# Wave attention: the value products of four heads in one call, a fourth sine of key tile 0 summed on TensorE, and that tile's sums in two banks by turns

## The chip, the cores and the metric

One core of a Trainium2 chip runs the whole kernel. The metric is the device time in microseconds (us). Engines are named as in the profile: PE is TensorE (PEld its weight loads), DVE is VectorE, ACT is ScalarE, POOL is GpSimd, SP is SyncE.

## What is computed

Four blocks one after the other on x of shape (8, 512, 128): a first attention, a mixture of experts, a second attention, the mixture again. The change touches the first attention, whose weights are sigmoids of a sum of five sines of the scores:

```python
sim = jnp.einsum('bhid,bhjd->bhij', q, k) / jnp.sqrt(hd) / temp      # 8 x 16 heads, 512 x 512
scores = 0
for fi, freq in enumerate([31.0, 37.0, 41.0, 43.0, 47.0]):
    scores = scores + a[fi] * jnp.sin(TWO_PI * sim / freq + p[fi])   # a, p: one number per head
w = jax.nn.sigmoid(scores)
w = w / (jnp.sum(w, axis=-1, keepdims=True) + 1e-10)
out = jnp.einsum('bhij,bhjd->bhid', w, v)
```

## The kernel before

`wave_attention` works through 128 heads (n), in 32 groups of four (`HG`; g is the group, h the head in it). A head's scores lie as 128 key rows by 2048 columns: four key tiles (kt) of 512 queries. The order on each engine is written out by hand; a loop (`Fori`) takes two groups in a pass, and the engines meet at semaphores only.

- **TensorE**, per head n: scores of head n+2, tiles 0 and 1 (`make_scores`, L667, one 128x512 matmul a tile, into psS); then the sum of the first three sines (`PE_F`) in psA: for each sine f and tile one fp32 matmul with a diagonal matrix that holds the head's factor (L704; a matmul in fp32 is two passes in the trace, so x8 is four matmuls). After f = 0 come the scores of head n+2, tiles 2 and 3. Behind head 0 of a group stand the value products of heads 0 and 1 of the group before, behind head 2 those of heads 2 and 3 (`values`, L679): 9 output rows a head, at psO rows 0, 32, 64 or 96, the two heads by turns.
- **ScalarE**, per head n: five sines over 2048 columns (L772), each when its angle is there; behind the third and the fifth it takes half of head n+2's scores out of psS (L737), the first angle. Behind head 0 it does the four sigmoids of the group before (L754), behind head 3 the copy of psO (L761). For head 0 of a group it makes the last angle too (L747).
- **VectorE**, per head n: the angles of head n+1 (`make_angles`: a multiply-add, L822, called a turn, for each of the angles 1 to 4, and a shift, L847, called a cut, for all five), then the fourth and fifth sine of head n added to psA's sums (`add_sine`, L860): two additions of 1024 columns each, from psA to score and from score to score.
- **GpSimd** makes the diagonals (L641), three a head, from identity and parameters, and copies V and the parameters of the next group.

The semaphores that matter: `sine` (ACT to PE and DVE), `summed` (a half of psA is complete: PE to DVE and POOL), `added` (an addition is done: DVE to PE, which may overwrite that half of psA, and to ACT), `s_ps` and `s_ready` (psS full: PE to ACT; taken: ACT to PE), `weighed` (a sigmoid is done: ACT to PE), `out_ps` (value products done), `used` (a sine was summed). Below, an engine's "head 1" is its work for a head with h = 1.

Of the kernel before, what the change touches and what calls it, by code (L numbers as in the profile page):

```python
# [11 lines left out]
ALU = mybir.AluOpType  # L12
# [3 lines left out]
P = 128  # L16
B, L, D = 8, 512, 128
H, HD = 16, 8
QT = L // P
NT = B * QT  # L20
HG = 4
NG = B * H // HG
# [2 lines left out]
FREQS = (31.0, 37.0, 41.0, 43.0, 47.0)  # L25
NF = len(FREQS)
PE_F = 3
TWO_PI = 2.0 * float(np.pi)
E, HID = 8, 512
NE = E + 1  # L30
# [504 lines left out]
def wave_attention(nc, sb, ps, sem, a, V, ident, dram, params, bound):  # L535
# [11 lines left out]
    N = QT * L  # L547
    HALF = N // 2
    SR, AR = 2, 2 * HG
    DV_F = NF - PE_F  # L550
    ADDS = 2 * DV_F

    C_SPS, C_SREADY, C_TURNED, C_LAST, C_CUT, C_SINE, C_USED, C_SUMMED = 2 * 2 * HG, 2, 2 * HG * (NF - 1), 2 * HG, 2 * HG * NF, NF, 2 * PE_F, 4
    C_ADDED, C_DIAG, C_OUT, C_TAKEN, C_STORED = 2 * HG * ADDS, 2 * HG, 2, 1, 16
    with ExitStack() as c:
# [7 lines left out]
        score = sb(c, "score", [P, AR, N])  # L563
        par = sb(c, "par", [P, 2, 3, HG * NF])
        far = sb(c, "far", [P, 1], I32)
        diag = sb(c, "diag", [P, 2, PE_F, P])
        og = sb(c, "og", [P, L])
        Vg = sb(c, "Vg", [P, 2, QT, HG, VW])
        psS = ps(c, "psS", [P, 2, L])
        psA = ps(c, "psA", [P, QT, L])  # L570
        psO = ps(c, "psO", [P, L])
        qk_loaded = [sem(c, f"qk_loaded{i}") for i in range(2)]
        s_ps = sem(c, "s_ps")
# [50 lines left out]
        @block.gpsimd  # L624
        def _(pool):

            pool.tensor_copy(par[:, 0, :, :], params[:, 0, :, :]).then_inc(par_ready, 1)
            with pool.Fori(0, B) as b:
                for gi in range(GPB):
                    g, u = b * GPB + gi, gi % 2  # L630

                    pool.wait_ge(out_ps, g - 1 + C_OUT)
                    pool.sem_inc(pool_step, 1)
                    pool.tensor_copy(Vg[:, u, :, :, :], V[:, bass.ds(g, 1), :, :, :]
                                     .rearrange("p a q h d -> p (a q) h d")).then_inc(v_ready, 1)
                    pool.wait_ge(par_ready, g + 1)
                    for h in range(HG):

                        pool.wait_ge(summed, (g * HG + h) * 2 - 2 + C_SUMMED)
                        for f in range(PE_F):  # L640
                            ins = pool.tensor_tensor(diag[:, h % 2, f, :], ident[:],  # L641
                                                     par[:, u, 1, h * NF + f:h * NF + f + 1]
                                                     .to_broadcast((P, P)), ALU.mult)
                        ins.then_inc(diag_ready, 1)
                        if h == 1:

                            pool.wait_ge(added, g * HG * ADDS + C_ADDED)
                            pool.wait_ge(cut, g * HG * NF + C_CUT)
                            pool.sem_inc(pool_step, 1)
                            pool.tensor_copy(par[:, 1 - u, :, :], params[:, (gi + 1) % GPB, :, :]  # L650
                                             ).then_inc(par_ready, 1)
            pool.wait_ge(out_ps, NG - 1 + C_OUT)
            pool.tensor_copy(Vg[:, 0, :, :, :], V[:, NG, :, :, :]).then_inc(v_ready, 1)

        @block.tensor
        def _(pe):
            for credit, n in ((s_ps, C_SPS), (s_ready, C_SREADY), (turned, C_TURNED), (last_turned, C_LAST), (cut, C_CUT), (sine, C_SINE),
                              (used, C_USED), (summed, C_SUMMED), (added, C_ADDED), (diag_ready, C_DIAG),
                              (out_ps, C_OUT), (out_taken, C_TAKEN),
                              (out_stored, C_STORED)):  # L660
                pe.sem_inc(credit, n)

            def make_scores(n, u, h, half):
                pe.wait_ge(s_ready, n * 2 + half + C_SREADY)
                for k in range(2):
                    kt = half * 2 + k
                    mm = pe.matmul(psS[:, k, :], kp[:, u, h, kt * P:(kt + 1) * P], qp[:, u, h, :],  # L667
                                   start=True, stop=True)
                mm.then_inc(s_ps, 1)

            def values(g, slot, heads):
                if heads[0] == 0:
                    pe.wait_ge(v_ready, g + 1)
                    pe.wait_ge(out_taken, g + C_TAKEN)
                pe.wait_ge(weighed, g * HG + heads[-1] + 1)
                for kt in range(QT):
                    for h in heads:
                        row = h * (P // HG)
                        mm = pe.matmul(psO[row:row + VW, :],  # L679
                                       Vg[:, slot ^ 1, kt, h, :],  # L680
                                       score[:, slot * HG + h, kt * L:(kt + 1) * L],
                                       start=(kt == 0), stop=(kt == QT - 1), skip_group_check=True)
                if heads[-1] == HG - 1:
                    mm.then_inc(out_ps, 1)

            def pair(gg, last):
                for u in range(2):
                    g = gg * 2 + u
                    for h in range(HG):
                        n = g * HG + h  # L690
                        more = not (last and u == 1 and h >= HG - 2)
                        nu, nh = (u, h + 2) if h < HG - 2 else (1 - u, h + 2 - HG)
                        if more:
                            if nh == 0:
                                pe.wait_ge(qk_loaded[nu], (gg + 1 + u) * 32)
                            make_scores(n + 2, nu, nh, 0)
                        pe.wait_ge(diag_ready, n + 1 + C_DIAG)
                        for f in range(PE_F):
                            pe.wait_ge(sine, n * NF + f + 1 + C_SINE)
                            for kt in range(QT):  # L700
                                if f == 0 and kt % 2 == 0:

                                    pe.wait_ge(added, n * ADDS - ADDS + kt // 2 + 1 + C_ADDED)
                                mm = pe.matmul(psA[:, kt, :], diag[:, h % 2, f, :],  # L704
                                               wave[:, h % 2, f, kt * L:(kt + 1) * L],
                                               start=(f == 0), stop=(f == PE_F - 1), skip_group_check=True)
                                if f == PE_F - 1 and kt % 2 == 1:
                                    mm.then_inc(summed, 1)
                            if f < PE_F - 1:
                                mm.then_inc(used, 1)  # L710
                            if more and f == 0:
                                make_scores(n + 2, nu, nh, 1)
                        if h in (0, 2):
                            values(g, 1 - u, (h, h + 1))

            pe.wait_ge(qk_loaded[0], 32)
            for h in range(2):
                for half in range(2):
                    make_scores(h, 0, h, half)
            with pe.Fori(0, NG // 2 - 1) as gg:  # L720
                pair(gg, False)
            pair(NG // 2 - 1, True)
            for h in (0, 2):
                values(NG, 1, (h, h + 1))

        @block.scalar
        def _(act):
# [77 lines left out]
        def _(dve):  # L805
# [19 lines left out]
            def make_angles(n, u, h, gs, general):  # L825
# [4 lines left out]
                for f in range(NF + 1):  # L830
                    if f < PE_F - 1:
                        dve.wait_ge(used, (n - 2) * (PE_F - 1) + f + 1 + C_USED)
                    elif f == PE_F - 1:
                        dve.wait_ge(summed, (n - 2) * 2 + 2 + C_SUMMED)
                    elif f < NF:
                        dve.wait_ge(added, n * ADDS - 2 * ADDS + 2 * (f - PE_F + 1) + C_ADDED)
                    if (f or general) and (f < NF - 1 or (f == NF - 1 and (general or h not in ACT_LAST))):
                        make_turns(n, u, h, f, general)
                    if f:
# [7 lines left out]
                        dve.tensor_scalar(angle[:, h % 2, f - 1, :], at, 32 - FRAC, None,  # L847
                                          ALU.logical_shift_left).then_inc(cut, 1)

            def add_sine(n, u, h, f):  # L850
                dve.wait_ge(sine, n * NF + f + 1 + C_SINE)
                for half in range(2):
                    cols = slice(half * HALF, (half + 1) * HALF)
                    if f == PE_F:
                        dve.wait_ge(summed, n * 2 + half + 1 + C_SUMMED)
                        other = psA[:, half * 2:half * 2 + 2, :].rearrange("p a n -> p (a n)")
                    else:
                        dve.wait_ge(added, n * ADDS + (f - PE_F - 1) * 2 + half + 1 + C_ADDED)
                        other = score[:, u * HG + h, cols]
                    dve.scalar_tensor_tensor(  # L860
                        out=score[:, u * HG + h, cols], in0=wave[:, h % 2, f, cols],
                        scalar=par[:, u, 1, h * NF + f:h * NF + f + 1], in1=other,
                        op0=ALU.mult, op1=ALU.add).then_inc(added, 1)

            def pair(gg, last, general):
                for u in range(2):
                    g = gg * 2 + u
                    for h in range(HG):
# [6 lines left out]
                            make_angles(n + 1, nu, nh, ng * 2 * HG, general)  # L875
                        if h == 0:
                            dve.wait_ge(out_ps, g + C_OUT)
                        for f in range(PE_F, NF):
                            add_sine(n, u, h, f)


            dve.tensor_scalar(far[:], bound[:], FAR * min(FREQS) / HD, None, ALU.is_ge).then_inc(far_ready, 1)
# [1036 lines left out]
```

## Time and profile before

| | |
|---|---|
| median of 3 runs | 4277.99 us (4274.96 to 4281.38) |
| the profiled execution | 4281.09 us, span 4279.3 us |
| PE busy | 3602.2 us (84%), 27092 instructions |
| DVE busy | 3409.0 us (80%), 4519 instructions |
| ACT busy | 2868.0 us (67%), 2433 instructions |
| POOL busy | 1271.6 us (30%), 918 instructions |
| L704, matmuls into psA | 1445.5 us |
| L772, sines | 1181.2 us |
| L679, value products | 239.8 us |

Wave attention fills about 110 to 2085 us of the span. In the profile a group of instructions has its busy time, the mean duration of one, and behind the bar the idle time of its engine just before it, with what ended it. In a timeline each row is a start, a length, the engine, the line and the instruction; equal instructions one behind the other are one row, with their count, and a row's length runs to the end of its last instruction, which overlaps the next row's start a little. So lengths of work are taken below from start to start.

### The profile page before, as it was taken

Reading aid. Unit: us, or ns where it says so; the run is one execution under the profiler, and the core shown is the slowest. Engines: PE = TensorE matmul, PEld = TensorE weight load, DVE = VectorE, ACT = ScalarE, POOL = GpSimd, SP = SyncE. Lnnn points to the kernel's source line nnn. Section 1 sums busy time; section 2 is a strip of 40 time slices with the busy share of each in tenths; the row PEclk is TensorE's granted clock in tenths of the full one; section 3 lists DMA queues with packets and bytes.
Section 4 is the critical chain, followed back from the end, with each engine's and each line's share of the span. In section 5 each row is a group of like instructions: output and inputs, shape, how many; then the busy total and the mean of one; then the engine's idle time right before and its main releaser. Section 6 shows DMA issues by size and latency. Waiting matters only on the chain. (4 is left out here: it accounts for less than half of the span.)

```text
span 4279.3 us, 71834 instructions
## 1 busy us (share of the span) xinstructions
PE 3602.2 (84%) x27092; PEld 2304.4 (54%) x27092; DVE 3409.0 (80%) x4519; ACT 2868.0 (67%) x2433; POOL 1271.6 (30%) x918
## 2 busy tenths in 40 slices
PE   3799999999999999999658814999999999998890
PEld 2233333333333333333347814989989889987690
DVE  6899999999999999999465544777777777776662
ACT  3899999999999999999323313555565565654430
POOL 2111111112112121212003343544544544531245
PEclk8899999999999999999869957999999999998895
DMA  5000000000000000000221227222223223312022
GB/s 141 17 12 6 12 12 12 6 12 12 12 9 9 12 12 12 6 12 9 99 71 36 61 65 164 54 47 59 55 45 59 55 45 59 61 31 80 20 64 67
DMA packets 149707, 174.78 MB, mean 41 GB/s; under 512 B 63824, under 2 KB 124848, under 8 KB 141264
## 3 DMA queue, kind: packets, MB, share of 16 engines
q1 hardware_dynamic: 140752, 153.35, 15.5%
q0 software_dynamic: 8704, 17.84, 1.8%
q8 instruction: 186, 3.05, 0.3%
q14 instruction: 65, 0.53, 0.0%
HBM read 119.04 MB, written 52.10 MB: 40 GB/s over the span
## 5 line engine op out<-in xcount | busy, mean ns | idle before, releaser
L704 PE MATMUL psA<-wave,diag 128*128 128x512 f32 x3072 | 1445.5, 622 | 136.5 <-DVE score L860 86.7
L772 ACT ACTIVATE wave<-wave 128x2048 f32<-128x2048 int32 x640 | 1181.2, 1904 | 3.6 <-DVE wave L847 2.2
L704 PEld LDWEIGHTS psA<-wave,diag 128*128 128x128 f32 x3072 | 584.4, 197 | 897.5 <-issue 699.2
L1785 ACT COPY r<-psR 128x1024 f32<-128x1024 f32 x512 | 482.6, 1039 | 358.1 <-PE psR L1709 357.5
L641 POOL TENSOR_TENSOR diag<-ident,par 128x128 f32<-128x128 f32 x384 | 292.6, 788 | 1441.0 <-PE psA L704 1441.0
L1655 POOL COPY kb<-ks 48x2048 bf16<-48x2048 bf16 x128 | 486.4, 3800 | 638.2 <-DMA ks<-kb_parts 534.5
L822 DVE TENSOR_SCALAR wave<-s,par 128x2048 int32<-128x2048 int32 x480 | 612.1, 1275 | 0.0
L847 DVE TENSOR_SCALAR wave<-wave 128x2048 int32<-128x2048 int32 x512 | 609.3, 1215 | 0.0
L1822 DVE TENSOR_TENSOR S<-psR,r 128x1024 f32<-128x1024 f32 x256 | 313.5, 1225 | 290.1 <-PE psR L1724 272.0
L737 ACT ACTIVATE s<-psS,par 128x1024 int32<-128x1024 f32 x256 | 282.8, 1105 | 132.4 <-PE psS L667 132.4
L1794 ACT ACTIVATE W<-psR 128x1024 f32<-128x1024 f32 x256 | 252.2, 1040 | 150.7 <-PE psR L1733 150.7
L860 DVE SCALAR_TENSOR_TENSOR score<-wave,par,psA 128x1024 f32<-128x1024 f32 x256 | 317.7, 1272 | 39.2 <-PE psA L704 39.2
L860 DVE SCALAR_TENSOR_TENSOR score<-wave,par,score 128x1024 f32<-128x1024 f32 x256 | 316.4, 1275 | 0.0
L1733 PE MATMUL psR<-ident,S 128*128 128x128 f32 x2048 | 269.5, 289 | 48.6 <-DVE S L1837 47.6
L1837 DVE TENSOR_SCALAR S<-S,m 128x512 f32<-128x512 f32 x512 | 307.8, 674 | 2.3
L1830 DVE TENSOR_REDUCE mx<-S 128x8 f32<-128x1024 f32 x256 | 297.8, 1210 | 0.0
L1709 PE MATMUL psR<-qb,T 112*128 112x64 bf16 x4096 | 244.5, 248 | 41.3 <-POOL qb L1655 41.3
L1733 PEld LDWEIGHTS psR<-ident,S 128*128 128x128 f32 x2048 | 241.5, 149 | 66.7 <-DVE S L1837 56.5
L1724 PE MATMUL psR<-ident,r 128*128 128x128 f32 x2048 | 266.8, 273 | 0.0
L1709 PEld LDWEIGHTS psR<-qb,T 112*128 112x128 bf16 x4096 | 237.0, 126 | 45.1 <-issue 42.1
L1709 PE MATMUL psR<-kb,T 112*128 112x64 bf16 x4096 | 245.8, 247 | 17.2 <-POOL kb L1655 17.2
L1709 PEld LDWEIGHTS psR<-kb,T 112*128 112x128 bf16 x4096 | 233.5, 125 | 23.3 <-POOL kb L1655 19.9
(254 smaller groups left out, 4473.7 us busy)
## 6 DMA issues: line engine op xcount, KB each, us to landing
ks<-kb_parts SPq DMA_DIRECT2D x128, 384.0 KB, 5.9
qs<-qb_parts SPq DMA_DIRECT2D x32, 384.0 KB, 8.5
ys<-f_ys SPq DMA_DIRECT2D x36, 256.0 KB
wave_out<-og SPq DMA_DIRECT2D x33, 256.0 KB, 2.1
o<-wave_out SPq DMA_DIRECT2D x8, 1024.0 KB, 5.1
qp<-qa_parts SPq DMA_DIRECT2D x32, 192.0 KB, 3.5
kp<-ka_parts SPq DMA_DIRECT2D x32, 192.0 KB, 4.0
f_wu<-in_w_up SPq DMA_DIRECT2D x2, 2048.0 KB, 10.4
```

The lines of the kernel that those rows point to most:

```text
L704: mm = pe.matmul(psA[:, kt, :], diag[:, h % 2, f, :], wave[:, h % 2, f, kt * L:(kt + 1) * L], start=(f == 0), stop=(f == PE_F - 1), skip_g ...
L772: act.activation(wave[:, h % 2, f, :], angle[:, h % 2, f, :], ACT.Sin, scale=float(TWO_PI / 2.0 ** 32)).then_inc(sine, 1)
L822: dve.tensor_scalar(angle[:, h % 2, f, :], src, scalar, par[:, u, row, h * NF + f:h * NF + f + 1], ALU.mult, ALU.add).then_inc(turned if f ...
L847: dve.tensor_scalar(angle[:, h % 2, f - 1, :], at, 32 - FRAC, None, ALU.logical_shift_left).then_inc(cut, 1)
L860: dve.scalar_tensor_tensor(out=score[:, u * HG + h, cols], in0=wave[:, h % 2, f, cols], scalar=par[:, u, 1, h * NF + f:h * NF + f + 1], in ...
L1655: pool.tensor_copy(dst[rows, :, odd, :], src[rows, :, :].rearrange("r h (n two) -> r n h two", two=2)[:, :, :, odd]).then_inc(ready, 1)
L1709: mm = pe.matmul(out[:, 2 * (j % 8):2 * (j % 8) + 2, :], T[:, way, w:w + P], src[:, pair, :, :], start=(j % 8 == 0), stop=True, skip_group ...
L1733: mm = pe.matmul(slot[:, i, kt * P:(kt + 1) * P], S[:, 2 * j + i, kt * P:(kt + 1) * P], ident[:], start=(kt == 0), stop=True, is_transpose ...
L1785: act.copy(dst[:, :, k * CP:(k + 1) * CP].rearrange("p h (a n) -> p a h n", a=2), psR[:, n % RING, :, :].rearrange("p a (h n) -> p a h n", ...
L1822: dve.tensor_tensor(S[:, hs, kt * P:(kt + 1) * P], psR[:, n % RING, :, :].rearrange("p a (h n) -> p (a h) n", n=P), r2[:, hs, :], ALU.add) ...
L1830: dve.tensor_reduce(mx[:, hs, kt], S[:, hs, kt * P:(kt + 1) * P], AX.X, ALU.max).then_inc(maxed, 1)
L1837: dve.tensor_scalar(S[:, h, :], S[:, h, :], m[:, h:h + 1], None, ALU.subtract).then_inc(shifted, 1)
```

## The change

- `values` is called once a group, behind head 1 (`VALUES = 1`), for all four heads of the group before, heads by turns inside the loop over tiles.
- The fourth sine of key tile 0 is summed on TensorE: a fourth diagonal (`ALL_F`), one matmul more a head. Sines 1 and 2 take their tiles in the order 1, 2, 3, 0, so that tiles 1 to 3 are complete first.
- psA has five banks instead of four. Tile 0's sums go to bank 0 for even heads and to bank 4 for odd ones; they wait only for the additions of head n-2. Tiles 1 to 3 wait for the first addition of head n-1.
- VectorE's additions are three a head (`ADDS`): the fourth sine of tiles 1 to 3 (1536 columns), the fifth of tiles 1 to 3, the fifth of tile 0 (512 columns, from psA).

```diff
+ALL_F = 4
...
-    DV_F = NF - PE_F
-    ADDS = 2 * DV_F
+    VALUES = 1
+    ADDS = 3
...
-        diag = sb(c, "diag", [P, 2, PE_F, P])
+        diag = sb(c, "diag", [P, 2, ALL_F, P])
-        psA = ps(c, "psA", [P, QT, L])
+        psA = ps(c, "psA", [P, QT + 1, L])
...
-                        for f in range(PE_F):
+                        for f in range(ALL_F):
                             ins = pool.tensor_tensor(diag[:, h % 2, f, :], ident[:],
...
-            def values(g, slot, heads):
-                if heads[0] == 0:
-                    pe.wait_ge(v_ready, g + 1)
-                    pe.wait_ge(out_taken, g + C_TAKEN)
-                pe.wait_ge(weighed, g * HG + heads[-1] + 1)
+            def values(g, slot):
+                pe.wait_ge(v_ready, g + 1)
+                pe.wait_ge(out_taken, g + C_TAKEN)
+                pe.wait_ge(weighed, g * HG + HG)
                 for kt in range(QT):
-                    for h in heads:
+                    for h in range(HG):
...
-                        for f in range(PE_F):
+                        alone = 0 if h % 2 == 0 else QT
+                        for f in range(ALL_F):
                             pe.wait_ge(sine, n * NF + f + 1 + C_SINE)
-                            for kt in range(QT):
-                                if f == 0 and kt % 2 == 0:
-
-                                    pe.wait_ge(added, n * ADDS - ADDS + kt // 2 + 1 + C_ADDED)
-                                mm = pe.matmul(psA[:, kt, :], diag[:, h % 2, f, :],
+                            order = (0,) if f == PE_F else (0, 1, 2, 3) if f == 0 else (1, 2, 3, 0)
+                            for kt in order:
+                                if f == 0 and kt == 0:
+                                    pe.wait_ge(added, n * ADDS - 2 * ADDS + ADDS + C_ADDED)
+                                if f == 0 and kt == 1:
+                                    pe.wait_ge(added, n * ADDS - ADDS + 1 + C_ADDED)
+                                final = f == (PE_F if kt == 0 else PE_F - 1)
+                                mm = pe.matmul(psA[:, kt if kt else alone, :], diag[:, h % 2, f, :],
                                                wave[:, h % 2, f, kt * L:(kt + 1) * L],
-                                               start=(f == 0), stop=(f == PE_F - 1), skip_group_check=True)
-                                if f == PE_F - 1 and kt % 2 == 1:
+                                               start=(f == 0), stop=final, skip_group_check=True)
+                                if final and kt in (0, QT - 1):
                                     mm.then_inc(summed, 1)
...
-                        if h in (0, 2):
-                            values(g, 1 - u, (h, h + 1))
+                        if h == VALUES:
+                            values(g, 1 - u)
...
-            def add_sine(n, u, h, f):
...
+            def add_sines(n, u, h):
+                rest, most = slice(0, L), slice(L, N)
+                sums, alone = psA[:].rearrange("p a n -> p (a n)"), psA[:, 0 if h % 2 == 0 else QT, :]
+                dve.wait_ge(sine, n * NF + PE_F + 1 + C_SINE)
+                dve.wait_ge(summed, n * 2 + 1 + C_SUMMED)
+                add_sine(n, u, h, PE_F, most, sums[:, most])
+                dve.wait_ge(sine, n * NF + NF + C_SINE)
+                dve.wait_ge(added, n * ADDS + 1 + C_ADDED)
+                add_sine(n, u, h, NF - 1, most, score[:, u * HG + h, most])
+                dve.wait_ge(summed, n * 2 + 2 + C_SUMMED)
+                add_sine(n, u, h, NF - 1, rest, alone)
```

How this moves the instructions, on TensorE first, in the loop over groups. From the end of head 0 to the start of head 1, before (ISA and REGISTER_ALU rows are semaphore and register work; MATMUL rows name out<-in):

```order
L704 MATMUL psA<-wave,diag 128x512 x4
L699 REGISTER_ALU
L704 MATMUL psA<-wave,diag 128x512 x4
L673 REGISTER_ALU
L679 MATMUL psO<-score,Vg 9x512 x8
L664 ISA
L667 MATMUL psS<-qp,kp 128x512 x2
```

and in the changed kernel:

```order
L707 MATMUL psA<-wave,diag 128x512 x4
L699 REGISTER_ALU
L707 MATMUL psA<-wave,diag 128x512 x4
L699 REGISTER_ALU
L707 MATMUL psA<-wave,diag 128x512
L665 ISA
L668 MATMUL psS<-qp,kp 128x512 x2
```

The eight value products are gone from there, and one psA matmul, the fourth sine of tile 0, is new. From the end of head 1 to the start of head 2 on TensorE, before:

```order
L704 MATMUL psA<-wave,diag 128x512 x4
L699 REGISTER_ALU
L704 MATMUL psA<-wave,diag 128x512 x4
L695 ISA
L664 ISA
L667 MATMUL psS<-qp,kp 128x512 x2
```

and in the changed kernel:

```order
L707 MATMUL psA<-wave,diag 128x512 x4
L699 REGISTER_ALU
L707 MATMUL psA<-wave,diag 128x512 x4
L699 REGISTER_ALU
L707 MATMUL psA<-wave,diag 128x512
L673 REGISTER_ALU
L675 REGISTER_ALU
L679 MATMUL psO<-score,Vg 9x512 x16
L694 ISA
```

Sixteen value products stand there now, and the eight that stood behind head 2 are gone too. VectorE's additions of a head, before:

```order
L860 SCALAR_TENSOR_TENSOR score<-wave,par,psA 128x1024
L855 REGISTER_ALU
L860 SCALAR_TENSOR_TENSOR score<-wave,par,psA 128x1024
L851 REGISTER_ALU
L860 SCALAR_TENSOR_TENSOR score<-wave,par,score 128x1024 x2
```

and in the changed kernel:

```order
L853 SCALAR_TENSOR_TENSOR score<-wave,par,psA 128x1536
L864 REGISTER_ALU
L865 ISA
L853 SCALAR_TENSOR_TENSOR score<-wave,par,score 128x1536
L867 REGISTER_ALU
L853 SCALAR_TENSOR_TENSOR score<-wave,par,psA 128x512
```

Four additions of 1024 columns are three, of 1536, 1536 and 512, and the one that reads tile 0's bank comes last.

## Rows read from the trace of the kernel before

**Rows 1.** Busy time of a stretch: us, PE, PEld, DVE, ACT, POOL, PEclk, DMA

```profile
1000.00:1200.00 200.00, 182.77 (x467) 67.49 (x468) 197.02 (x169) 189.59 (x122) 38.73 (x46) 0.97 0.04 10
```

**Rows 2.** Groups by line: busy us, mean ns | idle before, releaser

```profile
L704 PE MATMUL psA<-wave,diag 128*128 128x512 f32 x3072 | 1445.5, 622 | 136.5 <-DVE score L860 86.7 <-ACT wave L772 47.1 <-issue 2.0
...
L860 DVE SCALAR_TENSOR_TENSOR score<-wave,par,psA 128x1024 f32<-128x1024 f32 x256 | 317.7, 1272 | 39.2 <-PE psA L704 39.2
...
L737 ACT ACTIVATE s<-psS,par 128x1024 int32<-128x1024 f32 x256 | 282.8, 1105 | 132.4 <-PE psS L667 132.4
...
L772 ACT ACT_TABLE_LOAD x47 | 60.3, 1283 | 0.8
```

**Rows 3.** Timeline of PE at four heads: start us, us, engine, line

```profile
128.37 5.45 PE L704 MATMUL psA<-wave,diag 128*128 128x512 f32 x8 [4.15 <-ACT wave L772]
...
149.42 5.16 PE L704 MATMUL psA<-wave,diag 128*128 128x512 f32 x8 [2.67 <-ACT wave L772]
...
330.87 3.69 PE L704 MATMUL psA<-wave,diag 128*128 128x512 f32 x8 [2.26 <-DVE score L860]
...
2031.79 3.26 PE L704 MATMUL psA<-wave,diag 128*128 128x512 f32 x5 [1.97 <-issue]
```

**Rows 4.** Timeline of DVE, one group of heads

```profile
1019.07 1.27 DVE L822 TENSOR_SCALAR wave<-s,par 128x2048 int32<-128x2048 int32 x1
...
1034.30 1.27 DVE L822 TENSOR_SCALAR wave<-s,par 128x2048 int32<-128x2048 int32 x1
...
1045.96 2.46 DVE L860 SCALAR_TENSOR_TENSOR score<-wave,par,score 128x1024 f32<-128x1024 f32 x2
...
1048.35 1.27 DVE L822 TENSOR_SCALAR wave<-s,par 128x2048 int32<-128x2048 int32 x1
```

**Rows 5.** Timeline of ACT, the same group

```profile
979.48 5.51 ACT L772 ACTIVATE wave<-wave 128x2048 f32<-128x2048 int32 x3
...
1031.44 1.12 ACT L737 ACTIVATE s<-psS,par 128x1024 int32<-128x1024 f32 x1 [3.36 <-PE psS L667]
...
1039.41 5.53 ACT L772 ACTIVATE wave<-wave 128x2048 f32<-128x2048 int32 x3
```

**Rows 6.** Timeline of PE, the same group

```profile
1002.57 5.26 PE L704 MATMUL psA<-wave,diag 128*128 128x512 f32 x8 [2.67 <-DVE score L860]
...
1015.36 0.60 PE L667 MATMUL psS<-qp,kp 48*128 48x512 bf16 x2
...
1015.89 3.70 PE L704 MATMUL psA<-wave,diag 128*128 128x512 f32 x8
...
1027.12 3.61 PE L679 MATMUL psO<-score,Vg 128*9 128x512 f32 x16
...
1030.66 0.60 PE L667 MATMUL psS<-qp,kp 48*128 48x512 bf16 x2
```

**Rows 7.** Timeline of ACT, the start of another group

```profile
857.21 1.28 ACT L772 ACT_TABLE_LOAD   x1
```

**Rows 8.** Groups by line, DVE additions of other stages

```profile
L1822 DVE TENSOR_TENSOR S<-psR,r 128x1024 f32<-128x1024 f32 x256 | 313.5, 1225 | 290.1 <-PE psR L1724 272.0
...
L1293 DVE TENSOR_TENSOR X<-X,f_pp 128x512 f32<-128x512 f32 x16 | 10.8, 678 | 40.0 <-PE f_pp L1427 39.9
```

**Rows 9.** Timeline of PE, the second attention

```profile
3031.03 3.68 PE L1733 MATMUL psR<-ident,S 128*128 128x128 f32 x16 [2.97 <-DVE S L1837]
...
3034.63 1.90 PE L1749 MATMUL psDO<-W,Vb 128*9 128x128 f32 x32
...
3036.46 2.05 PE L1733 MATMUL psR<-ident,S 128*128 128x128 f32 x16
...
3038.44 1.06 PE L1749 MATMUL psDO<-W,Vb 128*9 128x128 f32 x32
...
3039.43 1.75 PE L1733 MATMUL psR<-ident,S 128*128 128x128 f32 x14
```

**Rows 10.** Busy time of a stretch, as rows 1, early wave attention

```profile
128.00:130.00 2.00, 1.64 (x2) 0.84 (x3) 2.00 (x3) 2.00 (x3) 0.00 (x0) 0.50 0.00 0
```

More of the change, by code:

```diff
@@ L682, in values @@
                                        start=(kt == 0), stop=(kt == QT - 1), skip_group_check=True)
-                if heads[-1] == HG - 1:
-                    mm.then_inc(out_ps, 1)
+                mm.then_inc(out_ps, 1)
             def pair(gg, last):
@@ L722, in _ @@
             pair(NG // 2 - 1, True)
-            for h in (0, 2):
-                values(NG, 1, (h, h + 1))
+            values(NG, 1)
         @block.scalar
@@ L835, in make_angles @@
                     elif f < NF:
-                        dve.wait_ge(added, n * ADDS - 2 * ADDS + 2 * (f - PE_F + 1) + C_ADDED)
+                        dve.wait_ge(added, n * ADDS - 2 * ADDS + (1 if f == PE_F else ADDS) + C_ADDED)
                     if (f or general) and (f < NF - 1 or (f == NF - 1 and (general or h not in ACT_LAST))):
@@ L848, in make_angles, with add_sine @@
                                           ALU.logical_shift_left).then_inc(cut, 1)
-            def add_sine(n, u, h, f):
[L851 to L863, printed above, removed]
+            def add_sine(n, u, h, f, cols, other):
+                dve.scalar_tensor_tensor(
+                    out=score[:, u * HG + h, cols], in0=wave[:, h % 2, f, cols],
+                    scalar=par[:, u, 1, h * NF + f:h * NF + f + 1], in1=other,
+                    op0=ALU.mult, op1=ALU.add).then_inc(added, 1)
+            def add_sines(n, u, h):
[9 more added lines that the diff above has]
+                add_sine(n, u, h, NF - 1, rest, alone)
             def pair(gg, last, general):
@@ L877, in pair @@
                             dve.wait_ge(out_ps, g + C_OUT)
-                        for f in range(PE_F, NF):
-                            add_sine(n, u, h, f)
+                        add_sines(n, u, h)
             dve.tensor_scalar(far[:], bound[:], FAR * min(FREQS) / HD, None, ALU.is_ge).then_inc(far_ready, 1)
```

## The prediction

> **What bounds the kernel now.** I read the busy time by stretch first. In 200 us of wave attention [rows 1] VectorE is busy 197.02, ScalarE 189.59, TensorE 182.77: three engines near full, so the question is not who is busiest but who waits for whom. The groups by line [rows 2] give the waits: VectorE's additions waited only 39.2 us for psA in the whole kernel, ScalarE's copies 132.4 us for psS, that is for TensorE's score matmuls.
>
> Then the timelines of one group of four heads. "Group" below is the time from a point of one group to the same point of the next. The first group's head 1 starts its psA matmuls at 149.42, the last one's at 2031.79 [rows 3]: 31 groups in 1882.4 us, 60.72 each. The whole prediction is what a group costs, times 31.
>
> Two loops compete for this number.
>
> VectorE's own: a head takes 15.23 (1019.07 to 1034.30), the one that prepares head 0 of the next group, whose last angle ScalarE makes, 14.05 (1034.30 to 1048.35) [rows 4]. 3 x 15.23 + 14.05 = 59.74. The rest up to 60.72 is about its wait for psA, 39.2 in all.
>
> The other loop goes through ScalarE and TensorE, and VectorE is not in it. ScalarE starts the sines of head 0 at 979.48 [rows 5]; behind them it does the sigmoids of the group before, and only then head 1's first sine. TensorE's head 1 waits for that sine: its psA matmuls start at 1002.57 after 2.67 idle [rows 6]. (This row puts the idle down to VectorE; at 149.42 [rows 3] the same 2.67 is put down to the sine, and the code allows only these two.) That is 23.09 from 979.48. TensorE then works without a gap: head 1 until 1015.36 (12.79), head 2 until 1027.12 (11.76), the value products of heads 2 and 3 until 1030.66 (3.54). Head 3 opens with score matmuls, and ScalarE, which had stood 3.36 idle in the middle of its own head 3, goes on at 1031.44 and reaches the next group's first sine at 1039.41 (8.75 together). Sum: 23.09 + 12.79 + 11.76 + 3.54 + 8.75 = 59.93. In the first group of a loop pass an ACT_TABLE_LOAD of about 1.3 stands ahead of that first sine (857.21, [rows 7]); 47 such loads at L772 [rows 2], less 32 behind the sigmoids and one at the start, leave 14 between my two end points. So this loop is as long as VectorE's.
>
> **The change, part by part.**
>
> VectorE. Four additions of 1024 columns become two of 1536 and one of 512. Two at a time take 2.39 (1045.96 to 1048.35 [rows 4]), 1.195 each. The slope is from two PSUM-fed additions elsewhere, 1225 ns at 1024 columns and 678 at 512 [rows 8]: 0.547 per 512. So 2 x 1.74 + 0.65 = 4.13 against 4.78: 0.65 less a head, 2.6 a group. VectorE's loop falls to 57.1.
>
> Value products. Two calls of 3.54 become one. Whether four heads run side by side is answered by the second attention's products, which have that form: 32 matrix passes of 128 columns in 0.99 (3038.44 to 3039.43 [rows 9]). Two-head products here need 3.54 for 16 passes of 512 columns, that is 0.44 for two at once; the short ones by fours need 0.99 / 8 = 0.12 at a quarter of the columns, where a quarter of 0.44 is 0.11. So the one call costs 3.54 (at 0.12 x 4 x 8 it would be 4.0, the bound above), and TensorE gives up 3.54 a group. The Trainium skill (TensorE: Matmul & The Clock Gate, "Packing small matmuls") has three column tiles of 512 columns at 2.38 times the speed of one, 79% of the ideal. If four went at 79% of theirs, an estimate by that page is 0.9 more a group, some 29 us in all; the row at 0.99 speaks against it, and my sum goes by the row.
>
> Which 3.54 goes? Not the one on the path. The call after head 0 filled the time in which TensorE waits anyway for the sigmoids to end; the call after head 2 lay on the path. The single call now stands after head 1, and the path runs from head 1 through head 2 to the start of head 3. It stays at 3.54 there, and nothing is saved on the path.
>
> The fourth sine on TensorE. One matmul more per head. Head 2 has 12 of them in 11.23 less 0.53 for its second scores (1015.89 to 1027.12; 0.53 is 1015.36 to 1015.89 [rows 6]): 0.89 each, 3.6 a group, which TensorE's total can bear. But two stand on the path, in heads 1 and 2: **+1.78**. Its sine is never late: ScalarE makes it right behind the third, while TensorE does eight matmuls.
>
> Waits. Tile 0's sums alternate between two banks, so TensorE starts a head before VectorE has read the last; tiles 1 to 3 wait for the first addition, now 1.74 long instead of 1.27. VectorE may begin its additions after the 11th matmul instead of the 10th. Both lie on the loop TensorE-VectorE: 4.13 + four turns and five cuts (15.23 - 4.78 = 10.45) on one side, 12.65 (11.76 + 0.89) on the other, each under 15.5, the mean head of the forecast. At the tightest place, head 0, VectorE's first addition of head 3 ends about 13.6 after TensorE's head 3 began, and tile 1 wants it at 14.0. GpSimd makes four diagonals instead of three per head, a whole head ahead. Neither costs time. If the 0.4 were gone, a few tenths a group would come on top; the queue behind it is head 0's second scores and ScalarE's copy ahead of the sigmoids.
>
> The clock. TensorE's head 3 starts 8.75 before ScalarE's head 0, so heads 3 and 0 (12.65 each) and the first scores of head 1 (0.53) end 17.1 after it, and the sine comes at 23.09: **6.0 idle** where there was 2.67. After such idle times the granted clock is at its lower level, 1.2 GHz, in some groups (0.50 from 128 to 130 us [rows 10]) and not in others: eight passes took 3.69 after 2.26 idle at 330.87, but 5.16 at 149.42 and 5.45 at 128.37, after 2.67 and 4.15 [rows 3]. So a fall costs 1.46 to 1.75 at the nearest rows; I call it L. After 6.0 idle I expect it in every group and take the row with the longest idle, L = 1.7. Lower bound 0, the row at 330.87. Upper bound from the second attention [rows 9]: after 2.97 idle, L1733 took 3.60 instead of 1.98 and L1749 and what is behind it 1.83 instead of 0.99, 2.46 together.
>
> Sum: head 1 at the full clock is 12.79 - 1.56 = 11.23 from its first psA matmul. The new group is 59.93 - 1.56 + 1.78 + L = 60.15 + L, against 57.1 for VectorE. Over 31 groups 1864.7 + 14 x 1.3 + 31 L = 1882.9 + 31 L, where 1882.4 stands now: +0.5 + 52.7 = **+53**. The start is the same (head 1 of the first group waits for the same sigmoids) and so is the end (one product call stands behind the last sigmoid as before). The profiled run took 4281.1 (span 4279.3), the median is 4278.0; from the median, **4331**.
>
> **The rivals.**
>
> *VectorE is the bound (faster).* For it: 98.5% busy. The Trainium skill (Perfetto Trace Analysis, "Identifying the Most-Contended Engine") says that the engine with the highest occupancy is the one to optimize first, which is this change. Worked out from rows: if TensorE never held ScalarE up, a group would be ScalarE's own 59.93 - 3.36 + 14/31 x 1.3 = 57.2, about VectorE's 57.1: 31 x 3.5 = 109 less, 4169. The gain begins where TensorE's stretch from head 1's first matmul to head 3 (11.23 + 1.78 + 11.76 + 3.54 = 28.3, with L 30.0) falls under 28.3, and is whole at 24.7. Against it: every term of 28.3 is a row, and ScalarE's 3.36 idle shows that head 3 is late already. I give it 9%.
>
> *The clock does not fall (no change).* L = 0: +0.5, 4278 to 4280. The loop stays 60.15 even then. 8%.
>
> *Four heads do not run side by side (slower).* If the call took 7.1, 31 x 3.5 = 110 more on the path: 4441. 3%.
>
> **How the numbers follow.** 80% for the forecast's case with L from 0.9 to 2.46: 4306 to 4355, widened by the 0.4 above and by a packing somewhat under the row's. 4298 to 4376 leaves out the first and the last rival and most of the second. A measurement of this kernel can tell about 0.2% (8.6 us) from no change. Faster 0.09, within it 0.08, slower 0.83.
>
> **What would show it.** In the changed profile TensorE's wait for ScalarE's sine ahead of psA should go from 47.1 us to about 200, its wait for VectorE from 86.7 to nearly 0 [rows 2]. VectorE's wait for psA should rise from 39.2 to about 150, with its busy share of the stretch down to 93%. Head 1's first eight passes should take 5.1 to 5.5 in nearly each group, one product call of 32 passes 3.6, and the group 61.8. I am wrong if ScalarE's wait for psS is near zero, or a group is under 60.

## The result, and the profile after

The changed kernel took 4359.6 us (median, 4354.28 to 4367.83) beside 4279.7 for the kernel before: a ratio of 1.0189, 95% interval 1.0168 to 1.0210, so 72 to 90 us slower. The forecast was 4331 with 4298 to 4376: the direction and the range hold, the size (53 forecast, 80 measured) was too small by a third. The profiled execution spans 4352.6 us against 4279.3, 73.3 more.

The stretch that answers to [rows 1] (the same columns):

```profile
1000.00:1200.00 200.00, 179.29 (x480) 68.75 (x479) 184.68 (x149) 181.60 (x117) 40.76 (x58) 0.93 0.04 10
```
VectorE went from 197.02 to 184.68 of 200 us, 92%, and all three engines are less busy than before: there is more waiting, not more work. The groups by line that answer to [rows 2]:

```profile
L707 PE MATMUL psA<-wave,diag 128*128 128x512 f32 x3328 | 1572.4, 625 | 214.2 <-ACT wave L774 202.5 <-issue 11.7
...
L853 DVE SCALAR_TENSOR_TENSOR score<-wave,par,psA 128x1536 f32<-128x1536 f32 x128 | 231.3, 1807 | 154.0 <-PE psA L707 154.0
...
L739 ACT ACTIVATE s<-psS,par 128x1024 int32<-128x1024 f32 x256 | 283.1, 1106 | 204.6 <-PE psS L668 204.6
```
TensorE's wait for the sine ahead of psA rose from 47.1 to 202.5 us, and its wait for VectorE is gone from the row (86.7 before). VectorE's wait for psA rose from 39.2 to 154.0, ScalarE's for psS from 132.4 to 204.6. One group of heads on ScalarE, as [rows 5]:

```profile
1009.90 5.51 ACT L774 ACTIVATE wave<-wave 128x2048 f32<-128x2048 int32 x3
...
1064.69 1.11 ACT L739 ACTIVATE s<-psS,par 128x1024 int32<-128x1024 f32 x1 [1.49 <-PE psS L668]
...
1072.66 5.53 ACT L774 ACTIVATE wave<-wave 128x2048 f32<-128x2048 int32 x3
```
and on TensorE, as [rows 6], with the next group's head 1, and the first and the last head 1 of the stage, as [rows 3]:

```profile
149.41 6.11 PE L707 MATMUL psA<-wave,diag 128*128 128x512 f32 x8 [5.66 <-ACT wave L774]
...
1033.00 6.34 PE L707 MATMUL psA<-wave,diag 128*128 128x512 f32 x8 [7.37 <-ACT wave L774]
...
1039.28 0.60 PE L668 MATMUL psS<-qp,kp 48*128 48x512 bf16 x2
...
1047.73 3.62 PE L679 MATMUL psO<-score,Vg 128*9 128x512 f32 x32
...
1051.29 0.60 PE L668 MATMUL psS<-qp,kp 48*128 48x512 bf16 x2
...
1063.91 0.60 PE L668 MATMUL psS<-qp,kp 48*128 48x512 bf16 x2
...
1095.77 5.68 PE L707 MATMUL psA<-wave,diag 128*128 128x512 f32 x8 [5.97 <-ACT wave L774]
...
1101.39 0.60 PE L668 MATMUL psS<-qp,kp 48*128 48x512 bf16 x2
...
2103.50 2.90 PE L707 MATMUL psA<-wave,diag 128*128 128x512 f32 x3 [5.75 <-issue]
```
The loop closes as the prediction wrote it: 1009.90 to 1033.00 is 23.10; head 1 to 1047.73 is 14.73; the one call with 32 passes 3.56; head 2 to 1063.91 is 12.62; and back to ScalarE's next first sine at 1072.66, 8.75. Sum 62.76, which is 1072.66 - 1009.90. From 149.41 to 2103.50 are 31 groups of 63.03 us, against 60.72. That is 71.7 us of the 73.3; the other 1.6 lie outside these 31 groups. The 80 us between the two medians are 7 more, since the profiled run of the changed kernel was its fastest; in the second measurement of the changed kernel (e0 below) the medians lie 71.6 apart.

VectorE's additions in this group:

```profile
1011.94 1.80 DVE L853 SCALAR_TENSOR_TENSOR score<-wave,par,psA 128x1536 f32<-128x1536 f32 x1
...
1013.77 1.82 DVE L853 SCALAR_TENSOR_TENSOR score<-wave,par,score 128x1536 f32<-128x1536 f32 x1
...
1015.51 0.74 DVE L853 SCALAR_TENSOR_TENSOR score<-wave,par,psA 128x512 f32<-128x512 f32 x1
...
1016.17 1.28 DVE L824 TENSOR_SCALAR wave<-s,par 128x2048 int32<-128x2048 int32 x1
...
1046.12 1.81 DVE L853 SCALAR_TENSOR_TENSOR score<-wave,par,psA 128x1536 f32<-128x1536 f32 x1 [4.68 <-PE psA L707]
```
From start to start 1.83, 1.74 and 0.66, 4.23 a head instead of 4.78. The first waited 4.68 us for TensorE in head 1.

### The profile page after: what moved, and what is told of

It is laid out like the page before. It is cut to its first block and busy times, and to the rows that moved or that the text cites. A ratio compares the mean times of both kernels' runs of the same rounds, so it can differ in the third digit from the quotient of the medians.

```text
span 4352.6 us, 72376 instructions
## 1 busy us (share of the span) xinstructions
PE 3604.5 (83%) x27348; PEld 2334.9 (54%) x27348; DVE 3361.1 (77%) x4391; ACT 2868.2 (66%) x2433; POOL 1306.0 (30%) x1046
## 5 line engine op out<-in xcount | busy, mean ns | idle before, releaser
L707 PE MATMUL psA<-wave,diag 128*128 128x512 f32 x3328 | 1572.4, 625 | 214.2 <-ACT wave L774 202.5
L707 PEld LDWEIGHTS psA<-wave,diag 128*128 128x128 f32 x3328 | 637.6, 199 | 1049.9 <-issue 905.2
L642 POOL TENSOR_TENSOR diag<-ident,par 128x128 f32<-128x128 f32 x512 | 330.3, 676 | 1529.0 <-PE psA L707 1529.0
L824 DVE TENSOR_SCALAR wave<-s,par 128x2048 int32<-128x2048 int32 x480 | 625.1, 1302 | 0.0
L853 DVE SCALAR_TENSOR_TENSOR score<-wave,par,psA 128x1536 f32<-128x1536 f32 (+1 forms) x256 | 325.7, 1272 | 154.0 <-PE psA L707 154.0
L739 ACT ACTIVATE s<-psS,par 128x1024 int32<-128x1024 f32 x256 | 283.1, 1106 | 204.6 <-PE psS L668 204.6
L1737 PE MATMUL psR<-ident,S 128*128 128x128 f32 x2048 | 263.9, 285 | 47.1 <-DVE S L1841 46.1
L1737 PEld LDWEIGHTS psR<-ident,S 128*128 128x128 f32 x2048 | 236.0, 147 | 65.2 <-DVE S L1841 55.1
L756 ACT ACTIVATE score<-score 128x2048 f32<-128x2048 f32 x132 | 241.4, 1899 | 5.8 <-DVE score L853 5.4
```

The source lines that it names most:

```text
L642: ins = pool.tensor_tensor(diag[:, h % 2, f, :], ident[:], par[:, u, 1, h * NF + f:h * NF + f + 1] .to_broadcast((P, P)), ALU.mult)
L707: mm = pe.matmul(psA[:, kt if kt else alone, :], diag[:, h % 2, f, :], wave[:, h % 2, f, kt * L:(kt + 1) * L], start=(f == 0), stop=final, ...
L824: dve.tensor_scalar(angle[:, h % 2, f, :], src, scalar, par[:, u, row, h * NF + f:h * NF + f + 1], ALU.mult, ALU.add).then_inc(turned if f ...
L853: dve.scalar_tensor_tensor(out=score[:, u * HG + h, cols], in0=wave[:, h % 2, f, cols], scalar=par[:, u, 1, h * NF + f:h * NF + f + 1], in ...
L1737: mm = pe.matmul(slot[:, i, kt * P:(kt + 1) * P], S[:, 2 * j + i, kt * P:(kt + 1) * P], ident[:], start=(kt == 0), stop=True, is_transpose ...
```

## The experiments

"Group" is the time of one group of four heads in the steady part of the trace, read from GpSimd's copy of the parameters (L650, L651 and the like), which comes once a group; where two values alternate, it is their mean. The kernels ran in three batches (e1 to e4; e0 and e5 to e7; e1 again, e9 and e10), each on a chip of its own and beside the kernel before. Its median differs from batch to batch (4254.8, 4259.4 and 4290.4 us), so ratios are compared, not times. In the traces the kernel before has a group of 60.73, the changed one 63.1.

| kernel | fourth sine on TensorE | value products | group us | ratio to before, 95% interval |
|---|---|---|---|---|
| before | no | 2 calls, heads 0 and 2 | 60.73 | 1 |
| changed, again (e0) | yes | one call, head 1 | 63.15 | 1.0166 (1.0142 to 1.0190) |
| e2 | yes | 2 calls, heads 0 and 2 | 63.15 | 1.0179 (1.0147 to 1.0211) |
| e3 | no | one call, head 1 | 61.44 | 1.0062 (1.0039 to 1.0085) |
| e4 | no | one call, head 0 | 61.44 | 1.0067 (1.0047 to 1.0087) |
| e1 | yes | one call, head 0 | 59.3 | 0.9923 (0.9894 to 0.9952) |
| e1 again | yes | one call, head 0 | 59.3 | 0.9915 (0.9896 to 0.9935) |
| e5: changed, idle time filled | yes | one call, head 1 | 61.73 | 1.0077 (1.0052 to 1.0102) |
| e6: changed, 0.9 us more in head 2 | yes | one call, head 1 | 64.00 | 1.0234 (1.0203 to 1.0264) |
| e7: changed, 0.9 us more in head 0 | yes | one call, head 1 | 63.15 | 1.0165 (1.0141 to 1.0188) |
| e9: e4, idle times filled | no | one call, head 0 | 59.75 | 0.9942 (0.9925 to 0.9959) |
| e10: changed, one bank for tile 0 | yes | one call, head 1 | 68.27 | 1.0564 (1.0537 to 1.0592) |

**Is the loop through ScalarE and TensorE the bound?** e6 and e7 add the same four matmuls, once on its stretch and once off it. The base is e0.

> The changed kernel once more, beside the three that follow on the same chip: 1.019 of the kernel before, a group of 63.1 us in the trace.

```diff
+                        if h in {2: 4}:        # e7: {0: 4}
+                            pe.wait_ge(added, n * ADDS - ADDS + C_ADDED)
+                            for _ in range({2: 4}[h]):
+                                pe.matmul(psA[:, alone, 0:P], ident[:], ident[:], start=True, stop=True,
+                                          skip_group_check=True)
                         for f in range(ALL_F):
```

> The changed kernel with four more 128x128 matmuls (0.9 us) at the start of head 2, on the stretch. Loop theory: 0.9 us more a group, 64.0, 28 us more in all. Rival (TensorE has room, its work hides): as changed.

> The changed kernel with the same four matmuls at the start of head 0, off the stretch: TensorE stands idle behind it. Loop theory: the group stays at 63.0 to 63.1, the idle time ahead of head 1 is 0.9 shorter (5.1 and 6.5). Rival (TensorE's total work counts): 28 us more, like the run with them in head 2.

The timeline of TensorE in e6, the added matmuls at the start of head 2 and what follows, and then e7, the added matmuls in head 0 and head 1 of two groups behind its idle time:

```profile
1002.80 1.16 PE L701 MATMUL psA<-ident 128*128 128x128 f32 x8
...
1003.80 3.60 PE L712 MATMUL psA<-wave,diag 128*128 128x512 f32 x8
```
```profile
1013.97 1.16 PE L701 MATMUL psA<-ident 128*128 128x128 f32 x8
...
1034.09 6.35 PE L712 MATMUL psA<-wave,diag 128*128 128x512 f32 x8 [6.53 <-ACT wave L779]
...
1096.86 5.68 PE L712 MATMUL psA<-wave,diag 128*128 128x512 f32 x8 [5.12 <-ACT wave L779]
```
e0 came out as expected, with 63.15 and a ratio of 1.0166, whose interval reaches 1.019. The same 8 passes (1.00 us from 1002.80 to 1003.80) cost 0.85 a group in head 2, 64.00 against 63.15, and 29 to 30 us in all by ratios and medians; in head 0 they cost nothing, 63.15, and the idle time ahead of head 1 shrank from 7.37 and 5.96 to 6.53 and 5.12. TensorE's total work is not what counts, its place is. So the loop through ScalarE and TensorE bounds the changed kernel.

**Which part of the change costs?** e2 takes the value products back to the two calls:

```diff
-                        if h == VALUES:
-                            values(g, 1 - u)
+                        if h in (0, 2):
+                            values(g, 1 - u, (h, h + 1))
```

> The fourth sine, the two banks and the three additions, with the value products in two calls of two heads behind heads 0 and 2, as before. Loop theory: before's loop of 58.4 + 0.6 and two matmuls more, 1.78, is 60.8 + L; idle ahead of head 1 is about 2.4 us, so L is 0 to 1.7: about 62.0 a group, 4320 us. Rival (VectorE bounds, and only the moved call spoilt the gain): VectorE's 57.1 a group, about 4170 us.

It measured 63.15, as much as the whole change: once the fourth sine is on TensorE, with its banks and VectorE's shorter additions, one call behind head 1 or two calls make no difference, and the shorter additions bring nothing back. The forecast for the run was 62.0 since I thought the clock's loss small after a short idle time. The trace of e2, head 1 of two groups and the call behind head 0 ahead of the first:

```profile
1025.52 3.61 PE L680 MATMUL psO<-score,Vg 128*9 128x512 f32 x16 [1.15 <-ACT score L759]
...
1032.34 6.65 PE L709 MATMUL psA<-wave,diag 128*128 128x512 f32 x8 [2.67 <-ACT wave L777]
...
1095.40 5.39 PE L709 MATMUL psA<-wave,diag 128*128 128x512 f32 x8 [2.48 <-ACT wave L777]
```
After idle times of 2.67 and 2.48 us the eight passes took 6.65 and 5.39, that is L of 2.95 and 1.7, mean 2.3; 58.4 + 0.6 + 1.78 + 2.3 = 63.1.

e3 is the other part alone, in the kernel before:

```diff
-                        if h in (0, 2):
-                            values(g, 1 - u, (h, h + 1))
+                        if h == 1:
+                            values(g, 1 - u)
```

> The kernel before with only the value products changed: one call of four heads behind head 1. Loop theory: the call stays on the stretch with the same 3.5 us, and the one that filled the idle time ahead of head 1 is gone, so L is 2.0 to 2.6 in every group: 58.4 + 0.6 + 2.3 = 61.3 a group, about 4297 us. Rival (TensorE's total is what counts): 3.5 us a group less, not slower than 4280 us.

61.44, within 0.2 of the loop's sum. Head 1 of two groups in its trace:

```profile
1016.66 5.79 PE L702 MATMUL psA<-wave,diag 128*128 128x512 f32 x8 [7.15 <-ACT wave L769]
...
1077.16 6.26 PE L702 MATMUL psA<-wave,diag 128*128 128x512 f32 x8 [5.74 <-DVE score L857]
```
Doing four heads at once halves TensorE's work on the products and makes this kernel 0.6% slower: the call that stays is the one that is waited for, and the idle time ahead of head 1 grows to 7.15 and 5.74. Head 1's first passes are slow in every group of e3. In the kernel before they are slow (5.16 to 5.39) in 19 of the 32 groups; in the other 13 they take 3.7. Six groups of that trace last 59.74 or 59.75, which is VectorE's own loop: in the kernel before the two loops set the pace by turns, and the prediction, which took a group with a fall at head 1 for all of them, did not see that.

The parts do not add up: e2 alone costs 2.42 a group, e3 alone 0.71, both together 2.42.

**Does the call's place decide?** e1 is the changed kernel with one number changed:

```diff
-    VALUES = 1
+    VALUES = 0
```

> The changed kernel with the single call of the value products behind head 0 instead of behind head 1. Theory (the loop through ScalarE and TensorE sets the pace): the 3.56 us call leaves the stretch from head 1 to head 3. It cannot start before the last sigmoid, 19.8 us after ScalarE's first sine, so head 1's psA matmuls start at 23.9 instead of 23.1. A group is 23.9 + 12.1 (head 1) + 12.6 (head 2) + 8.75 + 0.65 (half a table load) = 58.1 + L, with L 1.7 to 2.3 since TensorE still stands idle 3 to 5 us ahead of the call: about 60.1, 2.9 less than the changed kernel's 63.0, so about 4270 us. Rival (what costs is the handshake with VectorE, or the fourth sine, and the place of the call does not matter): 4360 us, as changed.

> The changed kernel with the call behind head 0 again, in more rounds: 0.990 to 0.995 of the kernel before, a group of 59.3 us.

Faster than both kernels, in both measurements: by 0.8% than the one before, and by about 2.5% than the changed one if the ratios to before are divided (0.9915 / 1.0166). TensorE's timeline of e1 around the call with head 3 behind it and a later call, the stretch's busy times (columns as in [rows 1]), and GpSimd's copies one group apart:

```profile
1036.44 3.62 PE L679 MATMUL psO<-score,Vg 128*9 128x512 f32 x32 [1.91 <-ACT score L756]
...
1039.99 0.60 PE L668 MATMUL psS<-qp,kp 48*128 48x512 bf16 x2
...
1040.53 3.70 PE L707 MATMUL psA<-wave,diag 128*128 128x512 f32 x8
...
1068.09 2.84 PE L707 MATMUL psA<-wave,diag 128*128 128x512 f32 x6 [1.09 <-DVE score L853]
...
1212.98 5.32 PE L679 MATMUL psO<-score,Vg 128*9 128x512 f32 x32 [2.64 <-ACT score L756]
```
```profile
1000.00:1400.00 400.00, 372.35 (x1032) 139.25 (x1031) 392.26 (x319) 386.55 (x247) 79.53 (x121) 0.99 0.05 11
```
```profile
1025.95 1.02 POOL L651 COPY par<-params 128x60 f32<-128x60 f32 x1 [3.17 <-DVE score L853]
...
1084.31 1.02 POOL L651 COPY par<-params 128x60 f32<-128x60 f32 x1 [3.17 <-DVE score L853]
```
The call at 1036.44 waits 1.91 us for the last sigmoid and runs at the full speed of 3.55, head 1 follows without a wait, and the granted clock of the stretch is 0.99, against 0.94 in the same stretch of the changed kernel. In every second group the call waits 2.64, and in 11 of 14 of those it then takes 5.32: such a group lasts 60.7 instead of 59.1, 1.6 more. So L is 0 in most groups and 0.6 in the mean, where I had put 1.7 to 2.3. My sum with 0.6 is 58.7; the trace has 59.3. What is left is VectorE: TensorE waits for it again, 1.09 us in head 3 and 0.61 in head 0, and VectorE at 98% and ScalarE at 97% say that this version is close to their own work.

e4 asks the same without the fourth sine:

> The kernel before with one call of four heads behind head 0. Loop theory: the stretch loses 3.5 us and starts 0.9 later, 56.4 + L with L about 2 is less than VectorE's own 59.74, so VectorE sets the pace: 59.8 to 60.2 a group, 4250 to 4262 us. Rival (the place does not matter): as the kernel before or as the call behind head 1.

This missed: 61.44, slower than before, where the expectation had 59.8 to 60.2. Its trace shows the slow passes in three places, in the call behind head 0, in head 0 and in head 3, each in one of every two groups:

```profile
1011.91 5.19 PE L678 MATMUL psO<-score,Vg 128*9 128x512 f32 x32 [3.91 <-ACT score L751]
...
1058.34 5.40 PE L702 MATMUL psA<-wave,diag 128*128 128x512 f32 x8 [2.21 <-DVE score L857]
...
1105.02 6.51 PE L702 MATMUL psA<-wave,diag 128*128 128x512 f32 x8 [3.13 <-DVE score L857]
```
The call took 5.19 instead of 3.62, the eight passes of a head 5.40 and 6.51 instead of 3.70. e9 fills those three idle times with matmuls of the identity into a fifth bank and changes nothing else:

```diff
+            def fill(count):
+                for _ in range(count):
+                    pe.matmul(psA[:, QT, 0:P], ident[:], ident[:], start=True, stop=True,
+                              skip_group_check=True)
...
+                        if h in (0, 3):
+                            fill(9 if h == 0 else 12)
                         for f in range(PE_F):
...
                         if h == 0:
+                            fill((14, 11)[u])
                             values(g, 1 - u)
```

> The kernel before with one call behind head 0 (the run that came out slower than forecast, 61.4 us a group), with extra 128x128 matmuls in TensorE's three idle times (ahead of the call, of head 3 and of head 0), into a fifth bank. Theory (the clock that falls in those idle times made head 0, head 3 and the call late, and VectorE waited for them): without the falls VectorE's own 59.74 sets the pace, 59.8 to 60.2 a group, 40 to 50 us less than that run. Rival (the call's place delays head 1 and so VectorE whatever the clock does): 61.4 stays.

```profile
1038.94 10.29 POOL L650 COPY par<-params 128x60 f32<-128x60 f32 x1 [4.06 <-DVE score L865]
...
1098.69 10.30 POOL L650 COPY par<-params 128x60 f32<-128x60 f32 x1 [4.06 <-DVE score L865]
```
```profile
1000.00:1400.00 400.00, 393.31 (x1393) 180.88 (x1393) 400.00 (x343) 383.70 (x245) 122.17 (x95) 1.00 0.05 11
```
59.75 from group to group, VectorE busy 400.00 of 400 us, the granted clock 1.00. That is VectorE's own loop, which the prediction had added up as 59.74 from [rows 4]. So the order of e4 is good by 1.0 a group against the kernel before, and the slow passes take 1.7 away (61.44 - 59.75; the ratios, 1.0067 and 0.9942, say 53 us in all, which is 1.7 x 31). e9 came out a little faster than expected.

**What does the clock cost in the changed kernel?** e5 fills the idle time ahead of head 1:

```diff
+                        if h == 1:
+                            pe.wait_ge(added, n * ADDS - ADDS + C_ADDED)
+                            for _ in range((30, 24)[u]):
+                                pe.matmul(psA[:, alone, 0:P], ident[:], ident[:], start=True, stop=True,
+                                          skip_group_check=True)
                         for f in range(ALL_F):
```

> The changed kernel with 24 or 30 more 128x128 matmuls (5 to 6.5 us, into the free bank) in the idle time ahead of head 1's psA matmuls, so that TensorE's clock has no reason to fall. Their results are overwritten. Loop theory: L goes from 2.3 us a group to nearly 0 and nothing else moves: a group of 60.7 us, the same as the kernel before, 72 us less than changed. Rival (the clock is only a part of the wait for VectorE, which stays): no change against changed.

TensorE's timeline of e5 in head 1 (the fill, the first sine's matmuls, the second scores):

```profile
1012.96 6.96 PE L701 MATMUL psA<-ident 128*128 128x128 f32 x60
...
1020.32 3.70 PE L712 MATMUL psA<-wave,diag 128*128 128x512 f32 x8 [0.40 <-ACT wave L779]
...
1024.92 0.60 PE L668 MATMUL psS<-qp,kp 48*128 48x512 bf16 x2 [0.90 <-ACT s L744]
```
61.73: between the two expectations. The granted clock from 1000 to 1400 us is 1.00, against 0.94 in the changed kernel. The eight passes are back at 3.70, L is 0, but 0.90 us of new idle stands behind them, put down to ScalarE's copy L744. Head 1's second scores wait until ScalarE, which has just begun head 1 as well, has done three sines and the copy; at the slow clock that wait is hidden. So a fall of L costs the loop only L - 0.9 (2.3 - 0.9 is 1.4, and 63.15 - 61.73 is 1.42). The trace of the kernel before had shown it. This is the row of second scores behind the fast passes at 330.87 of [rows 3]:

```profile
335.39 0.60 PE L667 MATMUL psS<-qp,kp 48*128 48x512 bf16 x2 [0.83 <-ACT s L737]
```
**What are the two banks worth?**

```diff
-                        alone = 0 if h % 2 == 0 else QT
+                        alone = 0
...
-                                    pe.wait_ge(added, n * ADDS - 2 * ADDS + ADDS + C_ADDED)
+                                    pe.wait_ge(added, n * ADDS + C_ADDED)
```

VectorE's third addition reads the same bank.

> The changed kernel with tile 0's sums always in bank 0, so that tile 0 of a head waits for the last addition of the head before. In the changed trace VectorE's additions of head 2 end about 4.3 us behind the 11th matmul of that head and TensorE wants the bank 2.3 us behind it: 2 to 3 us more at head 3, which is on the stretch, and some at head 0: a group of 65.2 to 66.5 us. Rival (VectorE is never late, the second bank buys nothing): 63.1.

68.27, 5.1 more than changed and above the expected 65.2 to 66.5. TensorE's heads of one group:

```profile
1005.23 5.40 PE L707 MATMUL psA<-wave,diag 128*128 128x512 f32 x8 [2.28 <-DVE score L853]
...
1021.89 5.40 PE L707 MATMUL psA<-wave,diag 128*128 128x512 f32 x8 [2.27 <-DVE score L853]
...
1040.96 5.09 PE L707 MATMUL psA<-wave,diag 128*128 128x512 f32 x8 [4.68 <-ACT wave L774]
```
It waits 2.3 us for VectorE at two heads of a group (3 and 0), as worked out, but each wait is followed by slow passes, 5.40 instead of 3.70. So with tile 0's sums completed last, the second bank is what makes the fourth sine bearable at all. How the 5.1 divide between waits and clock was not tried apart.

**What the sums leave open.** Kernels whose clock falls come out equal more closely than their parts are. e0, e2 and e7 have 63.15 to 0.01 us, though TensorE idles 7.37 and 5.96, 2.67 and 2.48, and 6.53 and 5.12 us ahead of head 1; e3 and e4 have 61.44, though their slow passes stand in different places. Once the clock falls nowhere in the loop the group is another one (61.73 in e5, 59.75 in e9). So L is no price of its own place alone, and a difference of some tenths between two kernels whose clock falls is not the price of the edit between them: this bears on the 0.00 between e0 and e2. Why the groups are equal was not tried.

## Why the prediction was right, and where it was too small

- *The bound: right.* The loop of 23.1, head 1, head 2, the call and 8.75 is in the changed trace term for term, and e6 and e7 show directly that work on it counts and work beside it does not.
- *VectorE.* Forecast 0.65 less a head, measured 0.55 (4.23 from start to start): the two long additions step 1.83 and 1.74, not 1.74. As forecast it buys nothing in the changed kernel. It does buy something once the stretch is short: e1's 59.3 lies under the 59.74 of VectorE's old loop.
- *The value products.* One call at 3.56, forecast 3.54. The estimate by the Trainium skill (TensorE: Matmul & The Clock Gate, "Packing small matmuls"), 0.9 more, is not seen: four column tiles cost what two did. That the saved call was the one in the idle time is shown by e3.
- *The fourth sine.* +1.78 on the stretch; a head went from 11.76 to 12.62, so 1.72 by the trace.
- *The clock: the term that was mis-sized.* I took L = 1.7 from heads with up to 4.15 us of idle. After 5.97 us of idle it is 5.62 from the eight passes' start to the next row, after 7.37 it is 6.28, against 3.63: L is 1.99 and 2.65 by turns, mean 2.32. (A head at the full clock, from 1051.82 to 1055.45, has the 3.63.) (2.32 - 1.7) x 31 = 19 us; 53 + 19 = 72, and the stage grew by 71.7. The sign given for it, eight passes of 5.1 to 5.5, missed: in all groups but the last they took 5.57 to 6.35. The upper case of L = 2.46 had room for 2.32, but its time, 4355, lies under the measured median of 4359.6; that one is in the range by the widening to 4376, which was meant for other terms.
- *A wait that I left out.* The case "the clock does not fall" was priced at +0.5 us. By e5 it would have been a group of 61.73, 31 us more in all (its ratio says 33): slower too. So that rival would not have brought the time out the same, and its 8% and the range's low end of 4298 were too generous.
- *The group's time* was given as 61.8 in the list of signs, which forgot half a table load; the sum itself had 62.4.
- *The rival by occupancy* (the Trainium skill, Perfetto Trace Analysis, "Identifying the Most-Contended Engine"). The busiest engine at 98.5% was relieved by moving work to TensorE, and the kernel became slower. In e9 VectorE is busy 400.00 of 400 us and every group has the length of its own loop; at 98.5%, in the kernel before, six groups had. No run relieved VectorE without loading TensorE.

## What to carry to other kernels

When three engines are each above 90% busy, add up the closed loops of waits, not the engines: the loop of 59.93 us that spared VectorE was already as long as VectorE's 59.74, and 1.00 us of matmuls put on it cost 0.85 while the same work elsewhere was free. When two calls are merged, ask which of the two stood in idle time; merging kept the one on the loop, and moving it to the idle place turned 1.9% slower into 0.8% faster. Idle time that looks harmless on an engine whose clock can fall may be paid by what comes behind it: filling it with matmuls that nobody reads took 1.4 us off a group of the changed kernel (e5) and 1.7 off one of e4 (e9).

## What was unexpected of the hardware

The length of the idle time doesn't tell what the fall of the clock costs. Ahead of the very first psA matmuls TensorE is idle for the same 4.15 or 4.16 us in the kernels shown here; the eight passes took 5.45 us in the kernel before [rows 3], and in the changed kernel and e1:

```profile
128.36 6.40 PE L707 MATMUL psA<-wave,diag 128*128 128x512 f32 x8 [4.15 <-ACT wave L774]
```
```profile
128.69 6.67 PE L707 MATMUL psA<-wave,diag 128*128 128x512 f32 x8 [4.16 <-ACT wave L774]
```
6.40 and 6.67. In e2 2.67 us of idle cost more (6.65) than 5.97 us did in the changed kernel (5.68), and in e3 5.74 cost more (6.26) than 7.15 (5.79). In the steady part, though, each place has its value and keeps it (5.68 and 6.34 by turns from 590 to 1980 us of the changed trace). So one trace gives L for its own schedule, and a moved instruction can change it by a microsecond or more without touching the idle time.
